# Routing woven into attention, mixer and experts; cross attention's bias add and normalisation off GpSimd

## What is computed

```python
x = _layernorm(x + _L0_attn_ref(x, ...))                       # causal self attention, 16 heads
x = _layernorm(x + _L0_xattn_ref(x, ctx_1024, ctx_1024, mask, ...))  # cross attention
x = _layernorm(x + _L0_ffn_ref(x, Wg, W1, W2, W3))             # 8 experts, each token goes to 2
x = _layernorm(x + _L1_attn_ref(x, ...))                       # a recurrent memory
x = _layernorm(x + _L1_xattn_ref(x, ctx_1024, ctx_1024))       # mixer: gelu(x W1) W2
x = _layernorm(x + _L1_ffn_ref(x, Wr, br, W1, b1, W2, b2))     # 8 experts, each token goes to 1
```

```python
scores = jnp.einsum('bsd,ed->bse', x, Wg)
topk_scores, topk_idx = jax.lax.top_k(scores, 2)
topk_probs = jax.nn.softmax(topk_scores, axis=-1)
# and, in the last layer
probs = jax.nn.softmax(xt @ Wr + br, axis=-1)
gate = jnp.max(probs, axis=-1)
idx = jnp.argmax(probs, axis=-1)
```

## Time and profile before

| | us |
|---|---|
| median of 3 runs | 1952.64 |
| the profiled execution | 1955.59 |
| its span | 1953.9 |
| PE busy | 1311.3 (67%) |
| DVE busy | 1370.8 (70%) |
| ACT busy | 1133.0 (58%) |
| POOL busy | 1030.3 (53%) |

### The profile page before, as it was taken

The page is one execution under the profiler, slowest core; times in us unless marked ns, Lnnn a source line. Parts: engine busy times, 40 slices in busy tenths (PEclk is TensorE's granted clock), DMA queues, the critical chain, the costliest instruction groups (busy, mean ns, idle before and its releaser), DMA issues. The chain is left out here.

```text
span 1953.9 us, 60466 instructions
## 1 busy us (share of the span) xinstructions
PE 1311.3 (67%) x18195; PEld 1070.9 (55%) x18196; DVE 1370.8 (70%) x4870; ACT 1133.0 (58%) x3308; POOL 1030.3 (53%) x1566
## 2 busy tenths in 40 slices
PE   6999995888858729996654999100000786849990
PEld 5777773666646618995653677100000565639990
DVE  5999994877787754453555666499999577755574
ACT  4777772777746616774554555365556565626674
POOL 3666664455559967777862444011111453867663
PEclk9999996999989969997886999655555898969995
DMA  3333331311112213333443454200000422323343
GB/s 88 98 94 97 97 98 41 112 49 49 51 45 72 69 44 91 97 97 116 135 136 93 89 109 83 41 1 1 1 1 5 153 67 62 86 59 90 88 114 115
DMA packets 192277, 148.11 MB, mean 76 GB/s; under 512 B 19458, under 2 KB 179586, under 8 KB 191746
## 3 DMA queue, kind: packets, MB, share of 16 engines
q1 hardware_dynamic: 178818, 118.93, 23.2%
q0 software_dynamic: 13312, 27.49, 4.3%
HBM read 76.54 MB, written 61.34 MB: 71 GB/s over the span
## 5 line engine op out<-in xcount | busy, mean ns | idle before, releaser
L1035 PE MATMUL ffn_run_up_ps<-ffn_run_xt,ffn_run_w_now 128*128 128x128 f32 x1792 | 250.5, 284 | 47.3 <-DVE ffn_run_h L1163 19.9
L1005 POOL DMA_INDIRECT expert_outputs<-ffn_run_y_all,ffn_run_ids x224 | 219.0, 978 | 87.6 <-issue 45.2
L1035 PEld LDWEIGHTS ffn_run_up_ps<-ffn_run_xt,ffn_run_w_now 128*128 128x128 f32 x1792 | 225.8, 198 | 59.1 <-ACT ffn_run_xt L1071 30.2
L778 POOL DMA_INDIRECT tokens_by_expert<-ffn_x_all,ffn_dest x192 | 192.8, 1004 | 52.6 <-issue 45.5
L1779 PE MATMUL mixer_m_ps<-mixer_mine,mem_state_coef 128*64 128x64 f32 x4 | 0.5, 334 | 284.2 <-DVE mixer_off_in L1913 284.2
L1044 PE MATMUL ffn_run_y_ps<-ffn_weights,ffn_run_h 128*128 x1216 | 174.0, 277 | 0.7 <-DVE ffn_run_y_all L1180 0.5
L1511 POOL TENSOR_TENSOR recur_rho<-recur_var_eps_new,k_pack 128x1 f32<-128x1 f32 x64 | 34.9, 545 | 248.4 <-DVE recur_var_eps_new L1605 248.4
L1779 PEld LDWEIGHTS mixer_m_ps<-mixer_mine,mem_state_coef 128*64 128x64 f32 x4 | 0.3, 206 | 284.3 <-DVE mixer_ones L1911 284.3
L1044 PEld LDWEIGHTS ffn_run_y_ps<-ffn_weights,ffn_run_h 128*128 128x128 f32 x1216 | 155.5, 194 | 1.1 <-issue 1.1
L1072 ACT COPY ffn_run_w_now<-ffn_weights 128x512 f32 x224 | 139.4, 622 | 0.1
L382 POOL TENSOR_TENSOR self_k_ex<-self_kt,k_pack 128x256 f32<-128x256 f32 x128 | 75.9, 614 | 116.7 <-ACT self_kt L569 116.7
(11 more groups left out here) (335 smaller groups left out, 4697.6 us busy)
## 6 DMA issues: line engine op xcount, KB each, us to landing
ffn_run_x<-tokens_by_expert SPq DMA_DIRECT2D x56, 260.0 KB, 2.9
tokens_by_expert<-fill_zeros SPq DMA_DIRECT2D x32, 292.5 KB, 2.8
ffn_run_yg<-expert_outputs SPq DMA_DIRECT2D x16, 512.0 KB, 4.7
memory_rows<-products_row SPq DMA_DIRECT2D x16, 390.0 KB, 4.6
ffn_weights<-memory_rows SPq DMA_DIRECT2D x16, 390.0 KB
tokens_by_expert<-fill_zeros SPq DMA_DIRECT2D x32, 162.5 KB, 2.6
ffn_weights<-in_pack_ffn SPq DMA_DIRECT2D x1, 4112.0 KB, 14.8
self_turned<-in_x_turned SPq DMA_DIRECT2D x64, 64.0 KB, 1.8
```

Source lines behind the costliest of these rows:

```text
L778: pool.indirect_dma_start(xs[h], bass.IndirectOffsetOnAxis(ap=self.dest[:, r, t:t + 1], axis=0), self.x_all[:, t, :], None)\
L1005: pool.indirect_dma_start(ys, bass.IndirectOffsetOnAxis(ap=ids[:, t:t + 1], axis=0), y_all[:, t, :], None)\
L1035: mm = nc.tensor.matmul(up_ps[t.slot(2)][:, c * P:(c + 1) * P], w_now[:, t.slot(2), c * P:(c + 1) * P], xt[:, t.slot(2), :], start=True, s ...
```

## The change

1. `route` is split into three parts: `select`, `keep_counts` and `place`. `select` and `place` are generators that give way after each operation. In cross DVE's step draws eight operations, two at each of four places; in the mixer six a step. Cross begins at step 37, the mixer at 35. The counts are copied out of PSUM (two copies of 128x256) instead of being read there. POOL's token scatters begin at step 43 instead of 40.
2. The second half's routing is no longer behind the last step of cross and mixer but inside `run_experts`: DVE draws six operations a step in its first 16 steps, PE counts in a new PSUM bank behind step 0, ACT's exponential comes at step 3 (first experts) or -2 (second). POOL waits for `routed` before its first scatter there, and every engine that needs the second half's experts waits for `experts_known`.
3. In cross the output bias comes with the residual: self attention writes its result a second time with cross attention's bias added (one more POOL add, one more store a tile), and cross loads `xr` from there. POOL's L364 is gone in cross, and so is the set-up of the bias.
4. In cross `y` is normalised by ACT with a scale and a shift; DVE makes the shift (128x1). POOL's L374 is gone there.

```diff
@@ attention, SP
-                    sp.dma_start(xr[:, t.slot(2), :], x_v[t.n]).then_inc(xr_in_sem[t.slot(2)], 16)
+                    sp.dma_start(xr[:, t.slot(2), :], res_v[t.n]).then_inc(xr_in_sem[t.slot(2)], 16)
...
+                    if not cross:
+                        sp.wait_ge(next_ready, t.count())
+                        sp.dma_start(next_v[t.n], y_next[:, t.slot(Y), :]).then_inc(stored[t.slot(Y)], 16)
@@ attention, POOL
-                if t.exists():
+                if t.exists() and not cross:
                     pool.wait_ge(xr_in_sem[t.slot(2)], t.uses(2) * 16)
...
+                t = i + -4
+                if t.exists() and not cross:
+                    pool.wait_ge(y_normed, t.count())
+                    if i.static and i.c == 4:
+                        pool.wait_ge(w_ready, 2)
+                    pool.tensor_tensor(y_next[:, t.slot(Y), :], y[:, t.slot(Y), :], bo_all[:, 1, :], ALU.add).then_inc(next_ready, 1)
...
-                    if i.c == middle:
+                    if i.c == begin + 6:
                         pool.wait_ge(f.routed, 1)
...
-                    if i.c < middle + HALF:
-                        f.scatter(pool, xs, 0, 2 * (i.c - middle))
-                        f.scatter(pool, xs, 0, 2 * (i.c - middle) + 1)
+                    if i.c >= begin + 6:
+                        f.scatter(pool, xs, 0, 2 * (i.c - begin - 6))
+                        f.scatter(pool, xs, 0, 2 * (i.c - begin - 6) + 1)
@@ attention, PE
+                    if f and i.static and i.c == begin + 2:
+                        f.count_tokens(pe, back, 0)
+                        pe.wait_ge(f.counts_read, 1)
@@ attention, ACT
+                t = i + -4
+                if t.exists() and cross:
+                    act.wait_ge(shift_ready, t.count())
...
+                    act.activation(y[:, t.slot(Y), :], r[:, t.slot(4), :], ACT.Identity, bias=shift[:, t.slot(4), :], scale=rstd[:, t.slot(4), :])\
+                        .then_inc(y_normed, 1)
@@ attention, DVE
+                if f and i.static and i.c == begin:
+                    routing.append(f.select(dve, 0))
+                if f and i.static and i.c == begin + 2:
+                    pull(64)
+                    f.keep_counts(dve, back, 0)
+                    routing.append(f.place(dve, 0))
...
+                pull(2)
...
-                half_way(dve, step, 4, 3, Tile, middle, lambda: f.route(dve, back, 0), peeled=8)
-                f.route(dve, back, 1)
+                half_way(dve, step, 4, 4, Tile, middle, peeled=8)
+                pull(64)
@@ Experts
+    def link(self, dve, ins):
+
+        self.links[0] += 1
+        ins.then_inc(self.chain, 1)
+        yield
+        dve.wait_ge(self.chain, self.links[0])
...
+    def keep_counts(self, dve, counts, h):
 
         dve.wait_ge(self.counted, h + 1)
-        link(dve.tensor_copy(full("total"), counts[:, 0:256].rearrange("p (t e) -> p t e", e=E_N)))
+        for n, name in enumerate(("total", "equal")):
+            cp = dve.tensor_copy(self.big[name][:, :, :].rearrange("p t e -> p (t e)"), counts[:, n * 256:(n + 1) * 256])
+        cp.then_inc(self.counts_read, 1)
@@ run_experts
+            pool.wait_ge(f.routed, 2)
             for n in range(K * HALF):
                 f.scatter(pool, xs, 1, n)
...
+                if i.static and i.c == 0:
+                    f.count_tokens(pe, counts, 1)
+            skewed(pe, step, 3, 0, kind, pause=(MID, lambda: pe.wait_ge(f.experts_known, 2)))
...
+                if i.static and i.c == (3 if top2 else -2):
+                    f.exponentials(act, 1)
...
+            routing = [f.select(dve, 1)]
+
+            def pull(n, i):
+                for _ in range(n if i.static and i.c < 16 else 0):
+                    next(routing[-1], None)
+
             def step(i):
                 e_now, e_ahead = (None, None) if top2 else look(i)
+                if i.static and i.c == 2:
+                    pull(64, i)
+                    f.keep_counts(dve, counts, 1)
+                    routing.append(f.place(dve, 1))
+                pull(3, i)
...
+                pull(3, i)
@@ memory_and_mixer
-        middle = NT // 2 + 8
+        middle, begin = HALF, HALF + 3
...
-                if i.c == middle:
+                if i.c == begin + 8:
                     pool.wait_ge(f.routed, 1)
...
                 for part in range(3):
+                    pull(2)
                     for n, t in enumerate((first, second)):
```

More of the change, by code:

```diff
@@ L3 @@
 from contextlib import ExitStack
+from functools import partial
 import concourse.bass as bass
@@ L265, in attention @@
         rstd = sb("rstd", [P, 4, 1])
+        shift = sb("shift", [P, 4, 1]) if cross else None
         Y = 4 if f else 2
+        PER = 16 if cross else 32
         y = sb("y", [P, Y, P])
@@ L517, in step @@
                     xq = xt[:, t.slot(2), :] if cross else xk
+                    if i.static and i.c == 0 and not cross:
+                        pe.wait_ge(k["later"], 32)
+                        pe.wait_ge(widened, 2)
+                        nc.tensor.matmul(b_next, bv_wide[:, 1, :], then["w"][:, 3 * P:], start=True, stop=False)
+                        nc.tensor.matmul(b_next, k["ones"][:, :], then["b_row"][0:1, :], start=False, stop=True)
                     nc.tensor.matmul(fk, w_t[:, 1, :], xk, start=True, stop=True)
@@ L572, in step @@
                     act.activation(qt[:, t.slot(2), :], fq, ACT.Identity, bias=b_cols[:, 0:1]).then_inc(q_copied, 1)
+                    if i.static and i.c == 0 and not cross:
+                        act.copy(bo_all[:, 1, :], b_next).then_inc(w_ready, 1)
                     if t.after(4):
@@ L813, in route @@
+            yield from link(stt(out=full("rest"), in0=sel[:, 0, :, :], scalar=-3.0e38, in1=full("ex"), op0=ALU.mult, op1=ALU.add))
+            yield from choose(1, full("rest"))
             tt(small["diff"][:, :], mx[:, 1, :], mx[:, 0, :], ALU.subtract).then_inc(self.exp_asked, 1)
             tt(self.sel_bf[:, :, :], sel[:, 0, :, :], sel[:, 1, :, :], ALU.add).then_inc(self.selected, 1)
+            yield
         else:
-            link(tt(full("rest"), logit, rows(self.b_gate[:, :]), ALU.add))
@@ L847, in route @@
-        link(tt(full("pos"), big[src][:, :, :], full("total"), ALU.subtract))
-        tt(full("pos"), full("pos"), counts[:, 256:512].rearrange("p (t e) -> p t e", e=E_N), ALU.add).then_inc(self.counts_read, 1)
-        dve.wait_ge(self.counts_read, h + 1)
-        link(tt(full("pos"), full("pos"), rows(self.base[:, :]), ALU.add))
+        yield from link(tt(self.base[:, :], self.ends[now][:, :], self.n_tiles[:, :], ALU.subtract))
+        yield from link(ts(self.base[:, :], self.base[:, :], float(P), None, ALU.mult))
@@ L1945, in norm, with pull @@
                     .then_inc(normed[n], 1)
+            routing = []
+            def pull(n):
+                for _ in range(n if routing else 0):
+                    next(routing[-1], None)
             def step(i):
+                if i.static and i.c == begin:
+                    routing.append(f.select(dve, 0))
+                if i.static and i.c == begin + 4:
+                    pull(64)
+                    f.keep_counts(dve, counts, 0)
+                    routing.append(f.place(dve, 0))
                 first, second = i + 3, i
@@ L1972, in step @@
                             statistics(n, t, part)
-            half_way(dve, step, 6, 1, Eights, middle, lambda: f.route(dve, counts, 0))
-            f.route(dve, counts, 1)
+            half_way(dve, step, 6, 1, Eights, middle)
+            pull(64)
 def build(nc, a, out):
```

199 lines of the change are left out of this document (113 added, 86 removed).

## The result

The changed kernel takes 2000.01 us (median of 4 runs) where the kernel before takes 1952.57: a ratio of 1.0241, with a 95% interval of 1.0223 to 1.0259. That is 47 us more, where 33 were forecast; the profiled execution has a span of 2000.9 us. That is the upper edge of the stated range, 1948 to 2000. The sign and the cause in the experts stages came as forecast. Cross attention, which was to give 14 us, took 5.

What follows compares the result with a forecast made beforehand. POOL's second-half scatter start was taken to bound the first experts: +14.6 us at its end, cross gain included, plus 18.2 in the second makes 32.8 on 1955.6, 1988.4; less 2.95 for the median, 1985.4 us, range 1948 to 2000.

Steps and rivals of the forecast that it cites:

- was to give 14 us: Cross attention: gain 15.9 us at the next block's start, less 2 for routing operations meeting POOL's.
- rival D: Cross and mixer: POOL operations hold woven routing up in full, or the weave hides nothing; 1992 to 2002 us, chance 0.08.
- first token scatter at +30.0: First experts: POOL waits for the second half's routing, starting scatters 30.0 us into the block instead of 1.44; +28.5 within the stage.
- A: Experts: TensorE, not POOL, ends the stages, so later scatters hide; 1936 to 1950 us, chance 0.12.
- B: Second experts: the stage absorbs its share, by slack over 8 us or the stop made good; 1970 us, chance 0.12.
- hide in idle time: Cross: ACT's norm (0.48 us) and DVE's shift (0.15) cost nothing beside idle time; without that cover 0.6 a tile.
- a loss of 14 us in six woven steps: Cross, steps 37 to 42: woven routing takes 45.3 us against 31.4 of SP's cadence; gain 3.5 over the unbroken block.
- 2 more for meetings with POOL: Cross: woven routing operations on DVE wait for POOL operations running beside them; 2 us lost.
- no cover: Same as rival D: 10.5 - 2 us more in cross and 9 - 1 in the mixer, or nothing hidden; chance 0.08.
- It was to give 5.4 us: Cross, second half: POOL's shorter tile gives 1.5 us over twenty tiles, 2.8 in the last seven, 1.1 from the add's lag.
- the next began 3.2 later: End of cross: the next block follows 3.2 us after the old block's end; added behind POOL's end for a start at 715.0.
- rival E: Self attention: slowed by SP's wait before the added store, up to 19 us; 2004 us, chance 0.03.

Runs made afterwards that it cites:

- the fourth run: Changed kernel with the in-stage routing of both experts stages drawn faster, up to 16 operations a step instead of 6; ratio 1.0229 to the kernel before.

## Why the prediction was right and wrong

The forecast was 1985.4 us, and 2000.01 was measured. The mechanism of the experts was right in both stages. That the time still lies at the edge of the range is luck in part: the range went up to 2000 for rival D, which did not come about, and what used the room was the end of cross attention and ACT's norm, for neither of which it was drawn.

**What the parts are worth**, from the ratios (times 1952.6; a step is uncertain by 2 to 4 us):

| | ratio | us for this step |
|---|---|---|
| weave alone | 0.9985 | -2.9 |
| and the bias fold | 0.9941 | -8.6 |
| and ACT's norm (part 2 undone) | 1.0007 | +12.9 |
| and the routing inside the experts (all of it) | 1.0241 | +45.7 |

**What bounds the experts: right.** The forecast put POOL's first token scatter at +30.0 in the first stage and about as much in the second; it came at +26.6 and +29.7. It put the loss within the first stage at 28.5, and 24.7 was measured (from 5.4 late to 30.1 late); in the second 21.6 against the stage's start, measured 19.7. The stop of DVE in the first stage is over 35 us as it said. That of the second is 8.82, not 15: DVE reaches the add of group 0 7.9 us later in the stage, where the forecast had 6.4 for that delay, and the add comes 16.8 later. The fetch was 19.7 later and not 21.6, and 2.9 us lie from it to the add, where 5.8 lay in the kernel before, in which nothing waited for it. Rivals A and B are out: POOL did not start before +17, undoing part 2 alone gave back 46 us, and the second stage lost its share. By the rows POOL sets the fetch, and in the fourth run a further slowed TensorE did not make the stages longer.

**Where a wait was added and none was counted.** That the ACT norm and DVE's shift "hide in idle time" is a step that failed. It compared ACT's busy time, 35 of 50 us, with the 0.48 added, and named neither what is queued behind the norm on ACT nor who waits for `y`. TensorE does, first thing in its step. The price without that cover was given as 0.6 us a tile and taken as nothing; measured are 0.28 in the settled tiles. With the norm on POOL r of tile 36 comes 185.4 us behind r of tile 0, in the changed kernel 198.4: 13.0 in the profile, and 12.9 in all by the ratios.

**The weave: too low.** The forecast had a loss of 14 us in six woven steps, and 2 more for meetings with POOL. From r of tile 35 to r of tile 43 the kernel before takes 61.3 us, the changed one 54.5: a gain of 6.8 where 1.5 was left after the 2 us for meetings (with the norm on POOL it takes 52.6, a gain of 8.7). The block in one piece cost more than the forecast had: at 5.24 a tile eight tiles are 41.9, so 19.4 were lost, not 16.5. The tile with the block took 22.46 us, the next 6.35, and the others 5.5, with POOL's scatters already in them. The six woven tiles took 43.4 us, not 45.3 and 2. The meetings are there: DVE and POOL in order of time, in the woven part,

```profile
545.09 0.58 DVE L866 TENSOR_SCALAR ffn_rest<-ffn_sel 128x256 f32<-128x256 f32 x1
...
552.27 0.48 DVE L870 TENSOR_TENSOR ffn_diff<-ffn_mx 128x32 f32<-128x32 f32 x1
...
544.89 1.25 POOL L392 TENSOR_TENSOR cross_k_ex<-cross_kt,k_pack 128x256 f32<-128x256 f32 x2 [4.16 <-ACT cross_kt L589]
...
552.08 1.48 POOL L392 TENSOR_TENSOR cross_k_ex<-cross_kt,k_pack 128x256 f32<-128x256 f32 x2 [5.43 <-ACT cross_kt L589]
```

DVE's two took 0.58 and 0.48 us where they take 0.29 and 0.19 in the unbroken block, and POOL's key expansions that met routing operations 1.25 and 1.48 instead of 1.17. For DVE these two are 0.6 us in all. Over the 51 routing operations that both kernels have, the woven ones took 0.1 us less than those in the block (one of which took 0.56 for 0.42), so 2 was too much. The rival "no cover", and with it the rule of the Trainium skill in "SBUF — State Buffer", section "SBUF: two separate sides", taken as a cost in every tile, did not come about: the second of DVE's rows, with two inputs from SBUF, agrees with the rule for single operations. The first has one input. That section has the lock for DVE operations in a 2-port perf mode as well, but in which mode this one ran no row says. Few operations met.

**The second half: too high.** It was to give 5.4 us from tile 43 to tile 63 and gave 0.7, with ACT's norm in the way. The same stretch is 107.1 us long in the kernel before, 101.8 with the norm on POOL again and 102.0 with ACT's norm ahead of the exponential, so some 5 us were there once the norm did not stand last in ACT's step.

**The end of the stage.** The step that failed here is "the next began 3.2 later", where it was carried over to POOL. The forecast took the 3.2 us from DVE's last routing operation to the next block and put it behind POOL's last scatter. Behind POOL it is 9.1 us: 727.2 to 736.4. The instructions at the end of cross attention's block (engine, operation, count: ns; when it began):

```profile
L241 DVEq DRAIN  x1: 199/199/199, 704.6 to 704.6; - x1
...
L241 POOLq DRAIN  x1: 20437/20437/20437, 712.1 to 712.1; - x1
```

POOL's drain ends at 712.1 + 20.4 = 732.5, 5.3 us after the last scatter's row ends, and then come 3.8 us in which SP clears the semaphores, 3.2 before. In the kernel before POOL was done 7 us ahead of DVE, and the drain, which went on for 5.3 us there too, was covered. The same in the mixer: POOL's last scatter ends at 1765.0 and the next block starts at 1770.3, 5.3 instead of 3.3. That is 2.0 of the 3.1 by which the stage's gain fell short (229.1 us became 228.8, where 3.4 were forecast); in the five kernels with this mixer and the routing inside the experts it takes 227.3 to 229.1, so the rest is within what differs from one execution to the next.

**The start.** Self attention loses 4.0 us in its first twenty tiles and nothing in the other 44, so rival E is out. How much of it is the change stays open: among runs with the same code for self attention the subtraction of tile 4 comes between 38.9 and 42.8 us, and in the run with self attention as before at 40.0, in the kernel before itself at 37.8. From self attention's last subtraction to r of tile 0 it is 43.9 us where it was 44.6: the bias set-up that is gone, less the added add and store, gives 0.6 and not 1.3.

**The sum.** The first experts start 5.4 later instead of 13.9 earlier: 19.3 us more than forecast. Of that, 12.1 had come by r of tile 63 (698.6 for 686.5, with the 2 us for meetings), 1.6 more by the end of POOL's last scatter, and 5.6 lie between that and the next block. The experts stages lose 24.7 + 19.7 instead of 28.5 + 21.6: 5.7 less (in each stage the delay of POOL was forecast a little long, and in the second its slack a little short). Memory and mixer give 1.2 and not 3.4: 2.2 more. Together 15.8, which is what lies between the fetch's 48.6 and the forecast's 32.8; 1.6 of it is given back behind the fetch (the span is 47.0 longer).

## What to carry to other kernels

Work that is moved in front of a queue of back-to-back DMAs costs the time by which it delays the queue's first instruction, less the slack of whoever waits for the queue (here 25 us of delay cost 25, and 29 with some 9 of slack cost 20), even where all engines have idle time beside it; ask first when the queue's first instruction can go. Before moving an operation to an idle engine, look not at that engine's busy share but at where the operation stands in its order and which engine has the result as its first need: the same 0.48 us cost 0.28 us a tile or nothing in the settled tiles. And when work is spread out, ask what is bound there: the weave paid where the block had stopped DVE, and was given back where POOL's scatters ended the stage.

## What the runs showed of the hardware

A block that ends with indirect DMAs issued by POOL is not over with their last row. POOL's drain lasted 5.3 us more after 64 scatters in cross attention and 2.7 more after 32 in the mixer, in the changed kernel and in the kernel before alike. Where DVE's work ends last, 3.2 us lie between the blocks in cross attention. Where POOL's drain ends last, it is 8.6 to 9.4 from the end of the last scatter's row to the next block, in all ten kernels with the routing woven.
